# The state's unit moved to the end of its group in the first part of a two-part attention kernel

## The chip, the cores and the metric

The kernel runs on one core of one Trainium2 chip. The metric is the device time of one execution in microseconds (us), the median of several. The core has TensorE (PE in the profile, with its weight loads as PEld), VectorE (DVE), ScalarE (ACT) and GpSimd (POOL); SyncE (SP) only issues DMAs here.

## The reference

The program adds three things: its input x, a linear attention over the layer-normed x, and a two-layer windowed transformer over the same. The change is in the linear attention only (8 sequences of 1024 tokens, 16 heads, 16 features a head):

```python
q = taylor_feature_map(q)      # [1, x/2, x*x/(4*sqrt 2), x_i*x_j/4]
k = taylor_feature_map(k)
kv = jnp.cumsum(k[..., None, :] * v[..., :, None], axis=2)
y = jnp.einsum('bhtD,bhtdD->bhtd', q, kv)
z = jnp.cumsum(k, axis=2)
denom = jnp.sum(q * z, axis=-1, keepdims=True) + EPS
y = y / denom
```

The feature map makes q.k a polynomial, so y can be had in two ways: by squared scores between tokens ("near", causal), or by a state, a small matrix summed over all tokens of the past that each later token is multiplied with.

## The kernel before

Two blocks run one after the other: `taylor_block` (0 to about 870 us of the span) and `transformer_block` (the rest, untouched). In `taylor_block` a batch is one sequence. PE, DVE, ACT, POOL and SP each have a program written out by hand, in a fixed order, tied by semaphores. A batch has a projection (`project`) and then `attention`, which takes its 16 heads in four groups (`GROUPS`, `GH`) of four heads; below, the groups of a batch are the first to the fourth.

A group is a list of 14 units (`UNITS`). Each unit takes a pair of PSUM banks, out of three pairs in turn (`RING = 3`, `unit_bank`), so a unit can start on PE only when the unit three places before it has been emptied (`consumed`). The units are

- ten "near" units (steps 0 to 4, two heads each): PE makes scores (L843), ACT squares them into `weights` (L687), DVE masks the diagonal blocks of each step (`mask_diagonals`, L464);
- one "state" unit (L801 on PE): the state of the first four tiles, out of `psi`. POOL writes the pair products into `psi` (`pairs`, L344), DVE the squares and the constant (`other_rows`, L492 to L501), ACT the linear rows (`linear_rows`, L664). DVE copies the state out (`keep_state`, L471), PE turns it (`turn_state`, L809 and L811) into the second bank of the unit, and DVE copies that out in two pieces (`turn_state`, L478 and L479). Only then are the unit's banks free (`state_ready`);
- two "past" units (L838), squared on ACT (L687), and one "rest" unit (L831), squared on ACT (L680).

Four units behind the scores PE multiplies a finished step's weights with the values (`attend`: L859 for the steps 0 to 4, L866 and L869 for the step of the past), one step after each last unit of a step. `psi` is written anew for each group, so POOL, DVE and ACT wait for `state_ps` (the state's last matmul) before they write it for the next group.

The units' numbers in a group, from 0, before: near 0 to 9, state 10, past 11 and 12, rest 13. Three places behind the state is the rest unit, so the rest unit waits for `state_ready`.

Two more things hang on this order. SP loads the heads of the fourth group (`load_heads`, 12 DMAs) behind `invert(b, 0)`, which waits for a reciprocal on DVE (`invert_den`, L397) that stands at the end of the second group's DVE program, behind `turn_state` and `other_rows`. And PE's first unit of a group waits for its heads to have landed (`qkT_in`).

Of the kernel before, what the change touches and what calls it, by code (L numbers as in the profile page):

```python
# [27 lines left out]
GROUPS, GH = 4, 4  # L28
# [7 lines left out]
FORMS = P + VP  # L36
# [26 lines left out]
def taylor_block(nc, B, x, wqk, wv, wo, ident, causal, earlier, eps_rows, keep_rows, forms, own_head, later, xn_d, attn_d, parts_d, xnT_d,  # L63
                 id_s, ao, rot, qks_s, last_stored):

    with ExitStack() as ctx:
# [3 lines left out]
        def sem(name):  # L70
# [35 lines left out]
        state_T = small[:, 0:FORMS]  # L106
# [71 lines left out]
        NS = len(STEPS)  # L178
# [2 lines left out]
        PIECE = SEQ // 4  # L181

        UNITS = [(kind, i, pair) for kind, i, pair in
                 [("near", i, pair) for i in range(NS) for pair in range(2)] + [("state", NS, 0)] +
                 [("past", NS, pair) for pair in range(2)] + [("rest", NS, 0)]]
        NU = len(UNITS)
        SQUARES = NU - 1

        def squares_to(n):
# [9 lines left out]
        def unit_bank(n):  # L199
            return 2 + 2 * (n % RING)  # L200
# [169 lines left out]
        def _(dve):  # L370
# [77 lines left out]
            def attention(b, following):  # L448
                def add_before(g, half):

                    tiles = slice(half * TILES // 2, (half + 1) * TILES // 2)
                    if g == 0 and half == 0:
                        dve.wait_ge(before_ready, b + 1)
                    dve.wait_ge(pv_done, (b * GROUPS + g) * AS + LAST_STEP[half] + 1)
                    v.tensor_tensor(yT[:, g, half * 512:(half + 1) * 512].rearrange("p (t n) -> p t n", n=P),
                                    ps[:, half, :].rearrange("p (t n) -> p t n", n=P),
                                    before[:, g, tiles].unsqueeze(2).to_broadcast([P, TILES // 2, P]), ALU.add).then_inc(yT_ready, 1)

                def mask_diagonals(g, i):
                    w = GH * ((g * AS + i) % RING)  # L460
                    dve.wait_ge(squared, (b * GROUPS + g) * SQUARES + 2 * i + 2)
                    for o, width in DIAGONALS[i]:
                        a = weights[:, w:w + GH, o:o + width]
                        last = v.scalar_tensor_tensor(a, a, 16.0, causal_s[:, 0:width].unsqueeze(1).to_broadcast([P, GH, width]),  # L464
                                                      ALU.add, ALU.mult)
                    last.then_inc(diag, 1)

                def keep_state(g):
                    group = b * GROUPS + g
                    dve.wait_ge(state_ps, group + 1)  # L470
                    v.tensor_copy(state_T, ps[:, unit_bank(g * NU + 2 * NS), 0:FORMS]).then_inc(state_kept, 1)  # L471

                def turn_state(g):
                    group, bank = b * GROUPS + g, unit_bank(g * NU + 2 * NS) + 1
                    dve.wait_ge(turned_ps, group + 1)
                    if group:
                        dve.wait_ge(pv_done, group * AS)
                    v.tensor_copy(state_main, ps[:, bank, 0:P])  # L478
                    v.tensor_tensor(state_rest, ps[:, bank, P:2 * P], own_s[:, 0:P], ALU.mult).then_inc(state_ready, 1)  # L479

                def other_rows(g):

                    group = b * GROUPS + g
                    if g == 0:
                        dve.wait_ge(krows_ready, PAST * (b + 1))
                        for half in parts_out:
                            dve.wait_ge(half, 16 * (BLOCKS // 2) * (b + 1))
                    if group:
                        dve.wait_ge(state_ps, group)
                    k = krows[:, g].rearrange("p t h d -> p (t h) d")  # L490
                    squares = psi[:, :, ROW_SQUARES:ROW_SQUARES + TD]
                    v.reduce_sum(ksum[:, :], k, AX).then_inc(ksum_ready, 1)  # L492
                    dve.wait_ge(ksum_ready, 4 * group + 1)
                    v.tensor_scalar_add(ksum[:, :], ksum[:, :], 1.0).then_inc(ksum_ready, 1)
                    dve.wait_ge(ksum_ready, 4 * group + 2)
                    v.scalar_tensor_tensor(squares, k, 2.0, ksum[:, :].unsqueeze(2).to_broadcast([P, PAST * GH, TD]), ALU.mult, ALU.subtract)\
                        .then_inc(ksum_ready, 1)
                    v.tensor_scalar(psi[:, :, ROW_ONE:FORMS], ksum[:, :].unsqueeze(2).to_broadcast([P, PAST * GH, FORMS - ROW_ONE]),
                                    -1.0 / (FORMS - ROW_ONE), 3.0 / (FORMS - ROW_ONE), ALU.mult, ALU.add).then_inc(ksum_ready, 1)
                    dve.wait_ge(ksum_ready, 4 * group + 4)  # L500
                    v.tensor_tensor(squares, squares, k, ALU.mult).then_inc(psi_rest, 1)  # L501

                for g in range(GROUPS):
                    mask_diagonals(g, 0)
                    if g >= 1:
                        add_before(g - 1, 1)
                    mask_diagonals(g, 1)
                    if following is not None and g <= 1:
                        for t in range(4 * g, 4 * g + 2):
                            tile_stats(following, t)  # L510
                    if following is not None and g >= 2:
                        layer_norm(following, 2 * (g - 2))
                        layer_norm(following, 2 * (g - 2) + 1)
                    if g >= 2:
                        spread_den(b, g - 2)
                    mask_diagonals(g, 2)
                    if following is not None and g <= 1:
                        for t in range(4 * g + 2, 4 * g + 4):
                            tile_stats(following, t)
                    if following is not None and g == 1:  # L520
                        variances(following)
                    if g >= 2:
                        keep_den(b, g - 2)
                    if g == 0:
                        other_rows(0)
                    mask_diagonals(g, 3)
                    keep_state(g)
                    mask_diagonals(g, 4)
                    turn_state(g)
                    add_before(g, 0)  # L530
                    if following is not None and g % 2 and b >= len(later):
                        scale_tables((b - len(later)) * 2 + g // 2)
                    if g + 1 < GROUPS:
                        other_rows(g + 1)
                    if g >= 1:
                        invert_den(b, g - 1)
                add_before(GROUPS - 1, 1)
                if following is not None:
                    for t in range(TILES // 2, TILES):
                        layer_norm(following, t)  # L540
                spread_den(b, GROUPS - 2)
                keep_den(b, GROUPS - 2)
# [25 lines left out]
        def _(act):  # L568
# [98 lines left out]
            def attention(b):  # L667
                first = b * GROUPS * AS
                for n in range(GROUPS * NU):
# [5 lines left out]
                    if kind == "rest":  # L675
# [2 lines left out]
                        if first + s >= AS:  # L678
                            act.wait_ge(pv_done, first + s - AS + 1)
                        a.activation(rest_w, ps[:, bank, :], ACT.Square, bias=own_s[:, P:P + 1]).then_inc(squared, 1)  # L680
                        if n // NU + 1 < GROUPS:
                            linear_rows(b, n // NU + 1)
                    else:
                        if pair == 0 and first + s >= RING:
                            act.wait_ge(pv_done, first + s - RING + 1)
# [2 lines left out]
                                     bias=four_s[:, :] if kind == "near" else zero_s[:, :]).then_inc(squared, 1)  # L688
                    if n == 5:
                        linear_rows(b, 0)  # L690

            project(0)
            for b in range(B - 1):
# [7 lines left out]
        def _(pe):  # L701
# [81 lines left out]
            def attention(b):  # L783
# [19 lines left out]
                    last.then_inc(state_ps, 1)  # L803

                def turn_state(g):
                    bank = unit_bank(g * NU + 2 * NS) + 1
                    pe.wait_ge(state_kept, b * GROUPS + g + 1)
                    for r in range(0, P, VP):
                        mm(ps[r:r + VP, bank, 0:P], state_T[:, r:r + VP], id_s[:, :], start=True, stop=True)  # L809
                    for r in range(0, P, VP):  # L810
                        last = mm(ps[r:r + VP, bank, P:2 * P], state_T[:, P:P + VP], id_s[:, :], start=True, stop=True)  # L811
                    last.then_inc(turned_ps, 1)

                def scores(n):
# [6 lines left out]
                        pe.wait_ge(before_ready, b + 1)  # L821
                    if n % NU == 0:
                        pe.wait_ge(qkT_in[g % 2], 16 * 2 * SLOTS * (2 * b + g // 2 + 1))
                    if b == 0 and n == 2 * NS + 1:
                        pe.wait_ge(forms_set, 1)
                    if kind == "state":
                        state(n)
# [47 lines left out]
                last_of = {}  # L875
                for n in range(units):
                    kind, i, pair = UNITS[n % NU]
                    last_of[n // NU, i] = n
                ends = {n: step for step, n in last_of.items()}
                for n in range(units + BEHIND):  # L880
                    if n < units:
                        scores(n)
                    if n - BEHIND in ends:
                        attend(*ends[n - BEHIND])
                    if n % NU == 2 * NS + 1 and n < units:
                        turn_state(n // NU)

            project(0)
# [953 lines left out]
```

## Time and profile before

| | |
|---|---|
| median of 3 runs | 3475.45 us (3474.73 to 3481.47) |
| profiled execution, its own time | 3475.38 us |
| its span | 3473.6 us |
| PE busy | 3330.0 us, 96% of the span |
| ACT, DVE, POOL busy | 2518.9, 2736.3 and 1536.3 us |
| mean granted TensorE clock | 0.991 of full speed |

The spans are of one execution. A busy matmul row includes the tail of its last matmul, so two rows that follow without a wait overlap by 0.15 to 0.2 us; the distance of two starts is the truer length. In the timeline a row merges neighbouring instructions of one kind, and shows in brackets how long the engine was idle before it and who released it.

### The profile page before, as it was taken

To read this page: it belongs to the slowest core of one execution; us is meant where nothing else is said; L and a number is where in the kernel's file an instruction comes from. 1 tells how busy PE (TensorE), PEld (TensorE's weight loads), DVE (VectorE), ACT (ScalarE), POOL (GpSimd) and SP (SyncE) were. 2 spreads that over 40 slices of the span, in tenths; PEclk is the share of its full clock that TensorE was granted. 3 is DMA by queue.
4 is the path that set the end of the run, shared out by engine and by line. 5 is a ranking of instruction groups with operands and counts; after the bars stand their busy time and mean duration, and the time that the engine had idled before them with its cause. 6 is when DMAs were issued, how large, how long until landed. Compare 5 with 4: busy or idle time off the path is not lost.

```text
span 3473.6 us, 96643 instructions
## 1 busy us (share of the span) xinstructions
PE 3330.0 (96%) x36960; PEld 2498.5 (72%) x36960; DVE 2736.3 (79%) x8256; ACT 2518.9 (73%) x5629; POOL 1536.3 (44%) x1547
## 2 busy tenths in 40 slices
PE   7898889887799999999999999999999999999999
PEld 4555545554588787788788788888788888888887
DVE  4767777777688888888888888888888888888886
ACT  5667776666577777777777777777777777777775
POOL 4444444444444444444444444444444444444443
PEclk9999999999899999999999999999999999999999
DMA  6756676654422222222222222222222222222211
GB/s 159 174 128 139 126 154 144 141 100 87 134 63 62 73 66 62 73 67 62 73 66 62 73 67 62 73 66 62 73 68 62 72 67 62 72 69 62 71 45 43
DMA packets 289965, 293.94 MB, mean 85 GB/s; under 512 B 40960, under 2 KB 221536, under 8 KB 288992
## 3 DMA queue, kind: packets, MB, share of 16 engines
q1 hardware_dynamic: 289504, 287.74, 34.7%
q8 instruction: 295, 4.83, 0.6%
q14 instruction: 166, 1.36, 0.1%
HBM read 104.89 MB, written 58.73 MB: 47 GB/s over the span
## 4 chain that ended last, share of the span: by engine, by line
PE 73%; DVE 1%; POOL 0%; ACT 0%; issue 0%; DMA 0%; SPq 0%; DVEq 0%; POOLq 0%
PE f_ps L1575 19%; PE f_ps L1683 16%; PE f_ps L1695 10%; PE f_ps L1660 6%; PE f_ps L1639 4%; PE f_ps L1580 3%; PE f_ps L1602 3%; PE f_ps L1620 3%; PE f_ps L1649 2%; PE f_ps L1609 2%; PE f_ps L1688 2%; PE f_ps L1624 2%; PE f_ps L1667 1%; PE f_ps L1561 0%; ACT pr L1491 0%
## 5 line engine op out<-in xcount | busy, mean ns | idle before, releaser
L1246 POOL TENSOR_TENSOR turned<-qk,rot 128x256 f32<-128x256 f32 x512 | 405.4, 813 | 1250.5 <-ACT qk L1458 1235.4
L1575 PE MATMUL f_ps<-wqkv_s,hT 128*128 128x512 f32 x1536 | 707.2, 596 | 8.9 <-DMA hT<-xnT_dram 5.5
L1683 PEld LDWEIGHTS f_ps<-hnT,w_s 128*128 128x128 f32 x5120 | 591.7, 192 | 63.0 <-issue 59.8
L1326 DVE CUSTOM_DVE_ANT_0 pr<-f_ps,masks_s 128x192 f32<-128x192 f32 x1024 | 326.4, 355 | 360.7 <-PE f_ps L1609 358.7
L1683 PE MATMUL f_ps<-hnT,w_s 128*128 128x128 f32 x5120 | 592.5, 275 | 2.5 <-DVE hnT L1383 2.5
L1491 ACT ACTIVATE pr<-pr,nmax,rnorm 128x192 f32<-128x192 f32 x1024 | 545.0, 535 | 44.4 <-DVE nmax L1333 44.4
L1575 PEld LDWEIGHTS f_ps<-wqkv_s,hT 128*128 128x128 f32 x1536 | 276.9, 191 | 273.6 <-issue 186.7
L1343 DVE TENSOR_SCALAR pr<-pr,rsum 128x192 f32<-128x192 f32 x1024 | 445.4, 497 | 9.0
L1695 PE MATMUL f_ps<-w_s,act_u 128*128 128x256 f32 x1536 | 352.7, 379 | 0.0
L687 ACT ACTIVATE weights<-t_ps,four_s 128x1024 f32<-128x1024 f32 x320 | 326.4, 1132 | 26.1 <-PE t_ps L843 26.1
L1253 POOL TENSOR_TENSOR rnorm<-ssq,f_mhalf 128x8 f32<-128x8 f32 x128 | 255.7, 1998 | 163.9 <-DVE ssq L1303 163.9
L1695 PEld LDWEIGHTS f_ps<-w_s,act_u 128*128 128x128 f32 x1536 | 281.9, 190 | 33.0
L1480 ACT ACTIVATE kT<-f_ps 128x512 f32<-128x512 f32 x128 | 76.4, 597 | 293.6 <-PE f_ps L1580 293.6
L1515 ACT ACTIVATE act_u<-f_ps,b_s 128x128 f32<-128x128 f32 x640 | 205.1, 364 | 105.1 <-PE f_ps L1688 90.2
L464 DVE SCALAR_TENSOR_TENSOR weights<-weights,causal_s 128x512 f32<-128x512 f32 (+1 forms) x192 | 200.3, 1058 | 94.6 <-ACT weights L687 94.3
L1660 PE MATMUL f_ps<-fwo_s,oT 128*128 128x256 f32 x1024 | 242.4, 380 | 0.4 <-ACT oT L1504 0.4
L1293 DVE TENSOR_TENSOR cosine<-qk,rot 128x512 f32<-128x512 f32 x256 | 209.3, 818 | 12.1 <-ACT qk L1458 11.6
L1393 DVE SCALAR_TENSOR_TENSOR act_u<-f_ps,b_s,act_u 128x128 f32<-128x128 f32 (+1 forms) x768 | 208.4, 340 | 6.7 <-ACT act_u L1515 4.2
L1260 POOL TENSOR_TENSOR rnorm<-ssq,f_mhalf 128x8 f32<-128x8 f32 x128 | 209.0, 1633 | 0.0
L843 PE MATMUL t_ps<-qkT 96*32 96x512 bf16 (+3 forms) x4096 | 177.0, 307 | 31.8 <-ACT weights L687 17.2
L1310 DVE TENSOR_TENSOR qk<-cosine,turned 128x512 f32<-128x512 f32 x256 | 206.7, 808 | 0.3 <-issue 0.3
L843 PEld LDWEIGHTS t_ps<-qkT 96*32 96x32 bf16 x4096 | 98.2, 98 | 144.2 <-issue 61.6
(151 smaller groups left out, 6873.5 us busy)
## 6 DMA issues: line engine op xcount, KB each, us to landing
vw<-vw SPq DMA_DIRECT2D x628, 128.0 KB, 2.5
qkT<-parts_dram SPq DMA_DIRECT2D x384, 128.0 KB, 5.7
kT<-kT SPq DMA_DIRECT2D x124, 256.0 KB, 2.7
parts_dram<-shared SPq DMA_DIRECT2D x64, 384.0 KB, 3.1
xnT_dram<-xnT SPq DMA_DIRECT2D x8, 1025.0 KB, 5.4
xs<-x_dram SPq DMA_DIRECT2D x8, 1024.0 KB, 7.4
xn_dram<-xn SPq DMA_DIRECT2D x8, 1024.0 KB, 5.0
attn_dram<-ao SPq DMA_DIRECT2D x8, 1024.0 KB, 9.6
```

The lines of the kernel that those rows point to most:

```text
L687: a.activation(weights[:, w:w + 2, :], ps[:, bank:bank + 2, :], ACT.Square, bias=four_s[:, :] if kind == "near" else zero_s[:, :]).then_in ...
L843: last = mm(ps[r:r + VP, bank + k, o:o + 512 - c], qkT[g % 2][:, 1, h, j * P + r:j * P + r + VP], qkT[g % 2][:, 0, h, half * 512 + c:(half ...
L1246: g.tensor_tensor(turned[:, heads, f], qk[:, heads, z], sines, ALU.mult).then_inc(done, 1)
L1253: g.tensor_tensor(rnorm[:, HEADS:], ssq[:, HEADS:], mhalf[:, HEADS:], ALU.pow).then_inc(knorm_ready, 1)
L1293: v.tensor_tensor(cosine[:, heads, :], qk[:, heads, :], table, ALU.mult).then_inc(done, 1)
L1326: last = v.tensor_tensor_reduce(out=chances(h), in0=ps[:, SCORES[p], k * 256:k * 256 + BAND], in1=mask_of(it)[:, HALF - k * HALF:HALF - k ...
L1343: last = v.tensor_scalar_mul(chances(h), chances(h), rsum[:, h:h + 1])
L1491: last = a.activation(chances(h), chances(h), ACT.Exp, bias=nmax[:, h:h + 1], scale=rnorm[:, h:h + 1], accum_out=psum[:, h:h + 1])
L1575: last = mm(ps[:, b, :], rows, wqkv_s[:, l, c, i * INNER:(i + 1) * INNER], start=(c == 0), stop=(c == KC - 1))
L1660: last = mm(ps[:, WO, 0:DIM], oT[:, c, :], wo_s[:, l, c, :], start=(c == 0), stop=(c == INNER // P - 1))
L1683: last = mm(ps[:, UP[j // 2], o:o + P], w1_s[:, l, c, half * FULL + j * P:half * FULL + j * P + P], hnT[:, c, :], start=(c == 0), stop=(c ...
L1695: last = mm(ps[:, DOWN, 0:DIM], act_u[:, j, :], w2_s[:, l, j, :], start=(j == 0), stop=(j == FB - 1))
```

## The change

The state's unit moves from place 10 to place 13, behind the past and rest units, and is counted as a step of its own. So past is 10 and 11, rest is 12. Three places behind the state is now the third unit of the next group. `turn_state` on PE follows the same unit's slot, behind the last near `attend`, and `attend` of the past comes one place earlier, behind the third near unit of the next group. On DVE `keep_state` comes behind `add_before(g, 0)`. On ACT the linear rows of a group are copied behind the second unit of that group, no longer behind the rest unit of the group before.

```diff
         UNITS = [(kind, i, pair) for kind, i, pair in
-                 [("near", i, pair) for i in range(NS) for pair in range(2)] + [("state", NS, 0)] +
-                 [("past", NS, pair) for pair in range(2)] + [("rest", NS, 0)]]
+                 [("near", i, pair) for i in range(NS) for pair in range(2)] + [("past", NS, pair) for pair in range(2)] +
+                 [("rest", NS, 0), ("state", AS, 0)]]
         NU = len(UNITS)
+        STATE = NU - 1
...
                     mask_diagonals(g, 3)
+                    mask_diagonals(g, 4)
+                    add_before(g, 0)
                     keep_state(g)
-                    mask_diagonals(g, 4)
                     turn_state(g)
-                    add_before(g, 0)
...
                         a.activation(rest_w, ps[:, bank, :], ACT.Square, bias=own_s[:, P:P + 1]).then_inc(squared, 1)
-                        if n // NU + 1 < GROUPS:
-                            linear_rows(b, n // NU + 1)
...
                     if n == 5:
                         linear_rows(b, 0)
+                    if n >= NU and n % NU == 1:
+                        linear_rows(b, n // NU)
...
                     kind, i, pair = UNITS[n % NU]
-                    last_of[n // NU, i] = n
+                    if kind != "state":
+                        last_of[n // NU, i] = n
                 ends = {n: step for step, n in last_of.items()}
                 for n in range(units + BEHIND):
                     if n < units:
                         scores(n)
                     if n - BEHIND in ends:
                         attend(*ends[n - BEHIND])
-                    if n % NU == 2 * NS + 1 and n < units:
+                    if n % NU == STATE and n < units:
                         turn_state(n // NU)
```

In the rows of the changed kernel the lines stand one higher (L801 is L802, L843 is L844), but for ACT's square of the near and past units (L687 is L686).

On PE, from the state's unit of the first group to the second group's first attend of the past, before:

```order
L801 MATMUL t_ps<-shared,vals 32x160 x16
L838 MATMUL t_ps<-qkT,forms_s 32x512 x8
L859 MATMUL t_ps<-weights,vals 32x256 x8
L809 MATMUL t_ps<-id_s,shared 32x128 x4
L811 MATMUL t_ps<-id_s,shared 32x128 x4
L838 MATMUL t_ps<-qkT,forms_s 32x512 x8
L831 MATMUL t_ps<-qkT,forms_s 32x512 x4
L859 MATMUL t_ps<-weights,vals 32x384 x4
L859 MATMUL t_ps<-weights,vals 32x128 x4
L843 MATMUL t_ps<-qkT 32x512 x32
L866 MATMUL t_ps<-weights,shared 32x512 x4
L869 MATMUL t_ps<-shared 32x512 x4
```

and the same stretch in the changed kernel:

```order
L839 MATMUL t_ps<-qkT,forms_s 32x512 x16
L860 MATMUL t_ps<-weights,vals 32x256 x8
L832 MATMUL t_ps<-qkT,forms_s 32x512 x4
L802 MATMUL t_ps<-shared,vals 32x160 x16
L860 MATMUL t_ps<-weights,vals 32x384 x4
L860 MATMUL t_ps<-weights,vals 32x128 x4
L810 MATMUL t_ps<-id_s,shared 32x128 x4
L812 MATMUL t_ps<-id_s,shared 32x128 x4
L844 MATMUL t_ps<-qkT 32x512 x24
L867 MATMUL t_ps<-weights,shared 32x512 x4
L870 MATMUL t_ps<-shared 32x512 x4
L844 MATMUL t_ps<-qkT 32x512 x8
```

State (L802) and turn (L810, L812) now stand between the last scores of the group (L832) and the first of the next (L844); the same instructions are there in both.

On DVE, the end of the second group, from the masks of its steps 3 and 4 to the reciprocal, before:

```order
L464 SCALAR_TENSOR_TENSOR weights<-weights,causal_s 128x4x128 x2
L471 COPY shared<-t_ps 128x160
L464 SCALAR_TENSOR_TENSOR weights<-weights,causal_s 128x4x256
L478 COPY shared<-t_ps 128x128
L479 TENSOR_TENSOR shared<-t_ps,own_s 128x128
L455 TENSOR_TENSOR yT<-t_ps,before 128x512
L492 TENSOR_REDUCE ksum<-krows 128x16
L494 TENSOR_SCALAR ksum<-ksum 128x16
L496 SCALAR_TENSOR_TENSOR shared<-krows,ksum 128x16x16
L498 TENSOR_SCALAR shared<-ksum 128x16x8
L501 TENSOR_TENSOR shared<-shared,krows 128x16x16
L397 RECIPROCAL den_flat<-den_flat 128x32
```

and changed:

```order
L465 SCALAR_TENSOR_TENSOR weights<-weights,causal_s 128x4x128 x2
L465 SCALAR_TENSOR_TENSOR weights<-weights,causal_s 128x4x256
L456 TENSOR_TENSOR yT<-t_ps,before 128x512
L472 COPY shared<-t_ps 128x160
L479 COPY shared<-t_ps 128x128
L480 TENSOR_TENSOR shared<-t_ps,own_s 128x128
L493 TENSOR_REDUCE ksum<-krows 128x16
L495 TENSOR_SCALAR ksum<-ksum 128x16
L497 SCALAR_TENSOR_TENSOR shared<-krows,ksum 128x16x16
L499 TENSOR_SCALAR shared<-ksum 128x16x8
L502 TENSOR_TENSOR shared<-shared,krows 128x16x16
L398 RECIPROCAL den_flat<-den_flat 128x32
```

The mask of step 4 and the add to `yT` moved ahead of the three copies of the state; the rows for the next group (L493 to L502) and the reciprocal still stand behind them.

## Rows read from the trace of the kernel before

**Rows 1.** Waits, 0 to 870 us: waiting engine and line <- releaser: total us, times, longest.

```profile
PEld t_ps L831 <- DVE shared L479: 31.2, 31, 2.3
PE t_ps L843 <- DMA qkT<-parts_dram: 14.0, 7, 5.8
```

**Rows 2.** Timeline of PE, fourth batch, second group to the fourth's start: start, length, instructions.

```profile
380.04 1.48 PE L843 MATMUL t_ps<-qkT 96*32 96x512 bf16 x24
...
389.24 1.26 PE L801 MATMUL t_ps<-shared,vals 128*32 128x160 f32 x32
390.33 0.61 PE L838 MATMUL t_ps<-qkT,forms_s 96*32 96x512 bf16 x8
...
391.85 0.43 PE L809 MATMUL t_ps<-id_s,shared 128*32 128x128 f32 x8
...
392.29 0.65 PE L838 MATMUL t_ps<-qkT,forms_s 96*32 96x512 bf16 x8
...
393.33 1.04 PE L859 MATMUL t_ps<-weights,vals 128*32 128x384 f32 x16
394.19 1.47 PE L843 MATMUL t_ps<-qkT 96*32 96x512 bf16 x24
...
410.68 0.61 PE L843 MATMUL t_ps<-qkT 96*32 96x512 bf16 x8 [1.87 <-DMA qkT<-parts_dram]
```

**Rows 3.** Timeline of ACT, the same second group.

```profile
380.70 10.15 ACT L687 ACTIVATE weights<-t_ps,four_s 128x1024 f32<-128x1024 f32 x10 [0.89 <-PE t_ps L843]
...
394.56 0.41 ACT L664 ACTIVATE shared<-krows 128x256 f32<-128x256 f32 x1
```

**Rows 4.** Timeline of DVE, the end of the same group.

```profile
392.56 0.29 DVE L478 COPY shared<-t_ps 128x128 f32<-128x128 f32 x1 [0.34 <-PE t_ps L811]
...
393.56 0.41 DVE L492 TENSOR_REDUCE ksum<-krows 128x16 f32<-128x256 f32 x1
...
396.11 0.35 DVE L397 RECIPROCAL den_flat<-den_flat 128x32 f32<-128x32 f32 x1
```

**Rows 5.** Timeline of PE, fifth batch, first group and the second's start.

```profile
467.21 1.48 PE L843 MATMUL t_ps<-qkT 96*32 96x512 bf16 x24
...
482.71 0.40 PE L831 MATMUL t_ps<-qkT,forms_s 96*32 96x512 bf16 x4 [1.42 <-DVE shared L479]
...
483.80 0.39 PE L843 MATMUL t_ps<-qkT 96*32 96x512 bf16 x3
```

**Rows 6.** Timeline of DVE, the same first group: masks of steps 3 and 4.

```profile
477.49 1.29 DVE L464 SCALAR_TENSOR_TENSOR weights<-weights,causal_s 128x512 f32<-128x512 f32 x2
...
479.42 2.84 DVE L464 SCALAR_TENSOR_TENSOR weights<-weights,causal_s 128x1024 f32<-128x1024 f32 x1
```

**Rows 7.** Timeline of POOL, the same stretch.

```profile
479.22 5.31 POOL L344 TENSOR_TENSOR shared<-krows 128x1024 f32<-128x1024 f32 x7 [3.64 <-PE t_ps L801]
```

**Rows 8.** Timeline of DVE, fifth batch, third group: mask of step 3.

```profile
508.80 1.82 DVE L464 SCALAR_TENSOR_TENSOR weights<-weights,causal_s 128x512 f32<-128x512 f32 x2
```

**Rows 9.** Timeline of PE, fifth batch, fourth group, to the next projection.

```profile
515.30 1.48 PE L843 MATMUL t_ps<-qkT 96*32 96x512 bf16 x24 [1.03 <-DMA qkT<-parts_dram]
...
530.25 1.06 PE L866 MATMUL t_ps<-weights,shared 128*32 128x512 f32 x8 [0.30 <-ACT shared L680]
...
532.11 0.66 PE L711 MATMUL t_ps<-id_s,xn 128*128 128x128 f32 x4
```

**Rows 10.** Timelines of PE: attention's first unit in batches two, six and eight.

```profile
153.41 0.83 PE L843 MATMUL t_ps<-qkT 96*32 96x512 bf16 x12
...
570.71 0.62 PE L843 MATMUL t_ps<-qkT 96*32 96x512 bf16 x8
...
784.40 0.83 PE L843 MATMUL t_ps<-qkT 96*32 96x512 bf16 x12
```

**Rows 11.** Windows, PE alone: stretch, us, busy (x), granted clock, DMA share, GB/s.

```profile
411.40:414.80 3.40, 3.40 (x32) 0.50 0.05 10
```

**Rows 12.** Timeline of PE, second batch, second group: idle without a releaser.

```profile
184.83 0.42 PE L859 MATMUL t_ps<-weights,vals 128*32 128x256 f32 x3 [2.76 <-issue]
```

More of the change, by code:

```diff
@@ L470, in keep_state @@
                     dve.wait_ge(state_ps, group + 1)
-                    v.tensor_copy(state_T, ps[:, unit_bank(g * NU + 2 * NS), 0:FORMS]).then_inc(state_kept, 1)
+                    v.tensor_copy(state_T, ps[:, unit_bank(g * NU + STATE), 0:FORMS]).then_inc(state_kept, 1)
                 def turn_state(g):
-                    group, bank = b * GROUPS + g, unit_bank(g * NU + 2 * NS) + 1
+                    group, bank = b * GROUPS + g, unit_bank(g * NU + STATE) + 1
                     dve.wait_ge(turned_ps, group + 1)
@@ L805, in turn_state @@
                 def turn_state(g):
-                    bank = unit_bank(g * NU + 2 * NS) + 1
+                    bank = unit_bank(g * NU + STATE) + 1
                     pe.wait_ge(state_kept, b * GROUPS + g + 1)
@@ L823, in scores @@
                         pe.wait_ge(qkT_in[g % 2], 16 * 2 * SLOTS * (2 * b + g // 2 + 1))
-                    if b == 0 and n == 2 * NS + 1:
+                    if b == 0 and n == 2 * NS:
                         pe.wait_ge(forms_set, 1)
```

## The prediction

> **What bounds the kernel now.** I read the waits of the first part, then PE's timeline over whole groups, then ACT's and DVE's beside it, and last the starts of the batches. The waits name the target: PE's loads for the rest unit stand 31.2 us in 31 of 32 groups for DVE's second copy of the turned state, and beside it PE waits 14.0 us in 7 places for the heads of a group [rows 1]. The first number is idle time of the load path; it is not yet time of a batch.
>
> A group without disturbance lasts 394.19 - 380.04 = 14.15 us [rows 2]. ACT squares the ten near units without a pause in 10.15 us, about 1.00 each with a tail of 0.12 [rows 3]; with two past units at 1.0, the rest unit at 0.6 and the linear rows at 0.3 (starts of the next instruction: 394.56 to the next square at 394.86) it needs some 13.1 us. PE has no more than 14.15 less its waits, about 13.0 us. So both are nearly full, and what decides is in which order they hand over. Groups start as follows: the fourth group of batch four waits 1.87 us for its heads and that of batch five 1.03 us [rows 2, 9]. The heads' loads are issued behind the reciprocal at 396.11 to 396.46, and the group starts at 410.68, 14.22 us later [rows 2, 4]. So the time from the second group's end to the fourth group's start is a chain through DVE's reciprocal and SP's loads, not through PE.
>
> **What the change costs and gives, group by group.** No instruction is added or taken away; only places move. I lay the rows end to end for one batch.
>
> *First group.* Before, 483.80 - 467.21 = 16.59 us, with 1.42 us of it in PE's wait for the state [rows 5]. The wait was long because DVE's mask of step 4 took 2.84 us beside POOL's pair products, which start as soon as the state is done [rows 6, 7], and the copies of the turned state stood behind it. Now that mask is ahead of the state, when POOL is idle. What is late next: the mask of step 3 ends at 477.49 + 1.29 = 478.78 [rows 6]. Behind it on PE come attend of step 3 (0.87), the rest unit (0.22), the state 390.33 - 389.24 = 1.09, attend of step 4 394.19 - 393.33 = 0.86 and the turn 392.29 - 391.85 = 0.44 [rows 2]: 3.5 us, so the second group starts at 482.3, after 15.1 us. Gain 1.5 us.
>
> *Second group.* The state now needs the bank pair of the first past unit, and everything of the next group stands behind the state. From the first scores: 0.66 to ACT's first square (380.04 to 380.70), 0.30 for the linear rows that are now between squares, 10.15 for the ten, 1.0 for the first past unit, 0.06 to PE, then 1.09 + 0.86 + 0.44 [rows 2, 3]: 14.6 us. Before, the same group took 14.15. The state's wait is gone (the turned state has two units' time, 0.87, and needs about 0.8: 0.27 from the turn's end to DVE's copy at 392.56, and the two copies), but ACT now starves through state, attend and turn. Loss 0.4 us.
>
> *Third group.* Its length is set by the load chain. DVE's first copy stands 0.27 us behind the turn's end in both [rows 2, 4]. Now the turn's end is also the group's start; `other_rows` (393.56 here, [rows 4]) comes 0.4 behind that copy, so 0.67 after the start where it was 0.63 ahead of it. From there to the reciprocal's end 396.46 - 393.56 = 2.9 us, since POOL's products run beside it as here. So the reciprocal ends 3.6 us after the third group's start, before it was 396.46 - 394.19 = 2.3. With 14.2 for the loads: 17.8 us, before 410.68 - 394.19 = 16.49. Loss 1.3 us. PE's own work of the group would be done at 14.6, so PE idles some 3 us for the heads where it had 1.87. The bounds of the delay: 1.3 at least (the order alone, POOL as before), and 2.6 if the first small operations are held up as mask 4 was, by 1.5 us [rows 6].
>
> *Fourth group.* Before, 532.11 - 515.30 = 16.81 us [rows 9]. Now 14.6 as above, and DVE's masks are later here: that of step 3 takes 1.82 us instead of 1.29 beside POOL [rows 6, 8] and the linear rows push the squares behind which DVE's other work stands; I put 0.5 for it. At the end nothing hides the turned state: 0.8, and then attend of the past, 532.11 - 530.25 = 1.86 [rows 9]. Together 17.7. Loss 0.9 us, between 0.3 and 1.3.
>
> **The sum.** 15.1 + 14.6 + 17.8 + 17.7 = 65.2 us for attention in a batch. Before, batch five took 532.11 - 467.21 = 64.90, and its whole period 570.71 - 467.21 = 103.50; the mean period over batches two to seven is (784.40 - 153.41) / 6 = 105.17 [rows 5, 9, 10], so the mean attention is 64.90 + 1.67 = 66.57. The difference holds two kinds of accident that 65.2 does not. One is PE idle without a releaser, 2.76 us in batch two [rows 12]; I see seven over 0.6 us in the eight batches, which made the second groups longer. They fall while the heads of the third group still land. I add 0.7 a batch, between 0 (they hide in ACT's backlog, now that the loads start earlier in the group) and 1.2. The other is the clock: behind the 1.87 us wait for heads PE ran 3.40 us at 0.50 of the clock, the lower level of 1.2 GHz [rows 11], which costs up to 1.7 us. That happened at 3 of the 8 fourth groups, with waits of 1.17 us and more; with 3 us of wait I expect it in 6 of 8, 1.4 each, so 1.1 a batch. That makes 67.0 against 66.57, and 8 x 0.4 = 3.5 us more. The profiled execution took 3475.38 us, and the median of the runs is 3475.45, so the forecast is 3479 us. The second part is not touched. It starts behind the last batch's tail, which moves with its fourth group; that is in the sum.
>
> The Trainium skill (SBUF — State Buffer, section "SBUF: two separate sides") says that VectorE and GpSimd share one pair of ports under an exclusive lock: an operation with two SBUF inputs blocks for the whole of the other engine's instruction. The 2.84 us mask agrees in kind [rows 6, 7]. By that rule the first mask of the next group could be held until POOL's 5.31 us are over, some 4.3 us after the group's start, and then be just late for its attend at 4.6; the sum would rise by up to 0.5 us a group.
>
> The Trainium skill (TensorE: Matmul & The Clock Gate, section "HAM oscillation — how this bites in real kernels") warns that a wait for a DMA in every pass of a loop lets the clock fall each time. The trace shows it in three of eight; by the rule it would be all eight, 2.8 us more in the sum.
>
> **The rivals.**
> *The load chain and the clock take more than the first group gives (slower).* Mechanism: DVE's reciprocal of the second group stands behind the copies of the turned state, so the fourth group's heads are late by 2 us instead of 1.3, and each wait is followed by half clock. Price: 0.7 + 0.35 a batch on top, and 0.4 for later masks: 1.4 x 8 = 11, so 3490 us. It decides from a reciprocal that ends more than 4 us after the group's start. For it: the chain has no slack in 7 places [rows 1]. Against: the small operations behind POOL took 2.9 us in all here [rows 4].
> *The gain stays (faster).* The accidents of the second group vanish, since the loads of the third group's heads are asked for 2 to 3 us earlier against PE, and the clock does not fall oftener: 65.2 + 0.5 = 65.7 a batch, 0.9 x 8 = 7 us less, and with the fourth group at its lower bound 12: 3464 to 3468 us. For it: the first group's 1.5 us are sure to reach the reciprocal. Against: the third group gives it back.
> *The wait only moves.* The third near unit of the next group now waits for the state's banks with a slack of 0.1 us (0.87 against 0.8). If DVE is late by 0.5 us there, PE waits in 24 groups: 12 us on top of the 65.2, less what ACT's starving hides, about 3485 us.
>
> **How the numbers follow.** No change that can be measured (within 0.2%, 7 us, which is about what a measurement of this kernel can tell) 0.43; the slower chain 0.30; the moved wait 0.07; the faster case 0.20. So faster 0.20, same 0.43, slower 0.37. The likeliest has 3472 to 3482. The range for 8 in 10 takes most of both sides, 3466 to 3491: below it lies the fourth group's lower bound together with no accidents, above it half clock at each fourth group and the 2.6 us delay.
>
> **What would show it.** In the changed profile the wait of the rest unit for DVE is gone, and none is at the third near unit. Second groups without an accident take 14.6 us, with ACT idle 1.5 us before each group's first square. First groups take 15.1. The reciprocal ends 3.6 us after the third group's start, and PE's wait for heads rises from 14.0 us to about 25. The fourth group takes 17.7 at full clock. I am wrong if the fourth group's start comes earlier against the batch's start by more than 1 us on the mean, or if DVE's masks, not ACT, set the state's start.

## The result: slower by 0.4%

| | before | changed |
|---|---|---|
| median | 3475.45 us (5 runs, 3468.55 to 3481.47) | 3488.51 us (5 runs, 3486.41 to 3493.75) |
| span of the profiled execution | 3473.6 us | 3484.6 us |

The ratio is 1.004, 95% interval 1.0024 to 1.0056, so 8 to 19 us more. The page of the changed kernel shows the same counts of instructions and slightly less work on DVE and ACT; the mean granted clock is 0.990 where it was 0.991:

```profile
PE 3341.7 (96%) x36960; PEld 2506.9 (72%) x36960; DVE 2720.8 (78%) x8256; ACT 2513.1 (72%) x5629; POOL 1528.3 (44%) x1547
```

The waits of the first part, changed kernel (0 to 870 us). The wait of the rest unit for DVE (31.2 us, [rows 1]) is gone, and what is left of it at the third unit is on the load path only; the wait for heads has doubled:

```profile
PE t_ps L844 <- DMA qkT<-parts_dram: 27.7, 9, 5.0
PEld t_ps L844 <- DVE shared L480: 3.4, 15, 0.2
```

PE's timeline, fourth batch, from the end of its first group to the start of its fourth (answers to [rows 2]):

```profile
380.97 1.07 PE L860 MATMUL t_ps<-weights,vals 128*32 128x256 f32 x16 [1.07 <-DVE weights L465]
381.83 0.43 PE L832 MATMUL t_ps<-qkT,forms_s 96*32 96x512 bf16 x4
382.05 1.30 PE L802 MATMUL t_ps<-shared,vals 128*32 128x160 f32 x32
383.13 1.08 PE L860 MATMUL t_ps<-weights,vals 128*32 128x384 f32 x16
384.00 0.43 PE L810 MATMUL t_ps<-id_s,shared 128*32 128x128 f32 x8
...
384.43 1.51 PE L844 MATMUL t_ps<-qkT 96*32 96x512 bf16 x24
...
399.18 1.51 PE L844 MATMUL t_ps<-qkT 96*32 96x512 bf16 x24
...
416.68 0.61 PE L844 MATMUL t_ps<-qkT 96*32 96x512 bf16 x8 [2.70 <-DMA qkT<-parts_dram]
```

The second group takes 399.18 - 384.43 = 14.75 us where it took 14.15, the third 17.50 where it took 16.49. ACT at the border of the first two groups: behind the rest unit's square it waits 2.14 us for the first scores, in place of 0.89 [rows 3]:

```profile
382.30 0.69 ACT L681 ACTIVATE shared<-t_ps,own_s 128x512 f32<-128x512 f32 x1
385.12 2.12 ACT L686 ACTIVATE weights<-t_ps,four_s 128x1024 f32<-128x1024 f32 x2 [2.14 <-PE t_ps L844]
```

DVE at the third group's start, 399.18 (answers to [rows 4]). The turned state is copied at 399.45, the reciprocal ends at 402.57, 3.39 us into the group; PE gets the heads 14.1 us behind it:

```profile
399.45 0.29 DVE L479 COPY shared<-t_ps 128x128 f32<-128x128 f32 x1 [0.97 <-PE t_ps L812]
...
400.80 0.82 DVE L497 SCALAR_TENSOR_TENSOR shared<-krows,ksum 128x256 f32<-128x256 f32 x1
...
402.23 0.34 DVE L398 RECIPROCAL den_flat<-den_flat 128x32 f32<-128x32 f32 x1
```

The fourth group of the fifth batch (answers to [rows 9]), and the clock at its start:

```profile
521.15 2.60 PE L844 MATMUL t_ps<-qkT 96*32 96x512 bf16 x24 [2.70 <-DMA qkT<-parts_dram]
...
538.01 1.07 PE L867 MATMUL t_ps<-weights,shared 128*32 128x512 f32 x8 [0.70 <-DVE shared L480]
...
539.87 0.66 PE L712 MATMUL t_ps<-id_s,xn 128*128 128x128 f32 x4
```

```profile
521.40:524.80 3.40, 3.40 (x32) 0.50 0.03 5
```

The table has the mean lengths of the groups over the eight batches, read as distances of such starts in one trace each. (Batch eight has no projection behind it; its fourth group is counted to the end of its last matmul, less the tail.) "Bubbles" are PE's idle times over 0.3 us that have no releaser, summed between 52 and 862 us. "Half clock" is the time in us that PE was granted 0.50 of its clock, up to the end of the last batch's groups, without the 6.8 us that every kernel has at the first batch's start. The projection between two batches takes 38.6 us in every kernel.

| | first | second | third | fourth | a batch | bubbles | half clock |
|---|---|---|---|---|---|---|---|
| before | 16.94 | 15.80 | 16.13 | 17.36 | 66.2 | 10.4 | 23.9 |
| changed | 15.60 | 15.40 | 18.13 | 18.68 | 67.8 | 4.0 | 34.1 |

Where the expectations below speak of 12.2 us of bubbles before, they count a wait of 1.8 us at 816.14 among them, which the profile puts down to DVE.

67.8 - 66.2 = 1.6 us in eight batches is 12.7 us. It is in the third and fourth groups: 2.0 and 1.3 us lost, 1.3 and 0.4 won in the first two.

### The profile page after: what moved, and what is told of

Its sections match the earlier page's. It is cut to its first block, busy times and chain, and to the rows that moved or that the text cites. A ratio compares the mean times of both kernels' runs of the same rounds, so it can differ in the third digit from the quotient of the medians.

```text
span 3484.6 us, 96643 instructions
## 1 busy us (share of the span) xinstructions
PE 3341.7 (96%) x36960; PEld 2506.9 (72%) x36960; DVE 2720.8 (78%) x8256; ACT 2513.1 (72%) x5629; POOL 1528.3 (44%) x1547
## 4 chain that ended last, share of the span: by engine, by line
PE 73%; DVE 1%; POOL 0%; ACT 0%; issue 0%; DMA 0%; SPq 0%; DVEq 0%; POOLq 0%
PE f_ps L1577 19%; PE f_ps L1685 16%; PE f_ps L1697 10%; PE f_ps L1662 6%; PE f_ps L1641 4%; PE f_ps L1582 3%; PE f_ps L1604 3%; PE f_ps L1622 3%; PE f_ps L1651 2%; PE f_ps L1611 2%; PE f_ps L1690 2%; PE f_ps L1626 2%; PE f_ps L1669 1%; PE f_ps L1563 0%; ACT pr L1493 0%
## 5 line engine op out<-in xcount | busy, mean ns | idle before, releaser
L686 ACT ACTIVATE weights<-t_ps,four_s 128x1024 f32<-128x1024 f32 x320 | 329.7, 1130 | 91.2 <-PE t_ps L844 91.2
L465 DVE SCALAR_TENSOR_TENSOR weights<-weights,causal_s 128x512 f32<-128x512 f32 (+1 forms) x192 | 180.1, 957 | 108.6 <-ACT weights L686 107.6
L844 PE MATMUL t_ps<-qkT 96*32 96x512 bf16 (+3 forms) x4096 | 189.1, 310 | 43.7 <-DMA qkT<-parts_dram 27.7
L844 PEld LDWEIGHTS t_ps<-qkT 96*32 96x32 bf16 x4096 | 103.8, 98 | 161.7 <-ACT weights L686 70.2
## 6 DMA issues: line engine op xcount, KB each, us to landing
attn_dram<-ao SPq DMA_DIRECT2D x8, 1024.0 KB, 10.2
```

The lines of the kernel that those rows point to most:

```text
L686: a.activation(weights[:, w:w + 2, :], ps[:, bank:bank + 2, :], ACT.Square, bias=four_s[:, :] if kind == "near" else zero_s[:, :]).then_in ...
L844: last = mm(ps[r:r + VP, bank + k, o:o + 512 - c], qkT[g % 2][:, 1, h, j * P + r:j * P + r + VP], qkT[g % 2][:, 0, h, half * 512 + c:(half ...
```

## The experiments

The theory is the load chain: DVE's reciprocal at the end of the second group gates SP's loads of the fourth group's heads; the change puts the reciprocal later. The rivals are ACT starving at the border of the groups, the moved ACT copy, and loads that are late by themselves.

**The reciprocal moved, in either kernel (e1, e2).**

```diff
                     mask_diagonals(g, 3)
+                    if g >= 1:
+                        invert_den(b, g - 1)
                     mask_diagonals(g, 4)
...
-                    if g >= 1:
-                        invert_den(b, g - 1)
```

(in e2 it stands behind `keep_state`, directly ahead of the same mask.)

> The changed kernel with one edit: DVE's reciprocal (invert_den) stands ahead of the mask of step 4, no longer behind the copies of the state and other_rows. Theory (load chain): the heads of the fourth group are then asked for behind the group's rest scores, about 2.5 us before the third group starts, and land 11 us into it, so PE's wait for them (27.7 us) goes and third groups fall from a mean of 18.1 us to about 14.8: 8 x 3.3 = 26 us. With the waits the half clock in 6 of 8 fourth groups goes, 1.4 us each, 8 us more. About 3488 - 34 = 3454 us. Rival (ACT starving at the group's border is the loss): the time stays above the kernel before, 3480 us or more, with third groups as long as now. Rival (the loads themselves are late, not their request): third groups stay at 17 us and more.

Measured 3458.26 us (3452.17 to 3461.33), ratio to the kernel before 0.9949 [0.9936, 0.9961]. That is 30 us below the changed kernel, from one DVE instruction of 0.34 us moved to another place in each group behind the first. No fourth group waits for heads; the only such wait left is at the start of the first batch:

```profile
PE t_ps L844 <- DMA qkT<-parts_dram: 4.6, 1, 4.6
```

```profile
390.05 1.51 PE L844 MATMUL t_ps<-qkT 96*32 96x512 bf16 x24
...
405.28 1.51 PE L844 MATMUL t_ps<-qkT 96*32 96x512 bf16 x24
```

The third group of batch four takes 15.23 us instead of 17.50; the mean is 15.20. Fourth groups fall to 17.56. Of the 3.7 us that a batch wins, 2.9 are in third groups and 1.1 in fourth groups. So the request for the heads was late, and not the loads by themselves, and ACT's starving is not the main loss.

> The kernel before with the same edit alone: the reciprocal ahead of the mask of step 4. Load chain: the waits for heads (14.0 us) go, third groups fall from 16.1 us to about 14.5, 13 us in all, and the half clock in 3 of 8 fourth groups goes, 4 us: about 3458 us. With e1 this tells what the new order of the units is worth without the load chain: by the rows (first group -1.3 us, second +0.4 where undisturbed, fourth +0.5) it comes out even, so e1 and e2 within 6 us of each other. Rival (the unit order is the real gain and only the chain hid it): e1 is 15 us or more below e2.

Measured 3478.67 us (3469.59 to 3482.70), ratio 1.001 [1.0001, 1.0019]: no gain, against 3458 expected. The waits for heads did go, but here the reciprocal stands too early. It waits for the denominators' DMA 16.4 us in 12 places, and the mask behind it meets POOL's products (2.07 us, where it takes 1.2 alone). DVE in the second group of batch five:

```profile
498.74 0.35 DVE L397 RECIPROCAL den_flat<-den_flat 128x32 f32<-128x32 f32 x1 [1.32 <-DMA den_flat<-yT]
499.01 2.07 DVE L464 SCALAR_TENSOR_TENSOR weights<-weights,causal_s 128x1024 f32<-128x1024 f32 x1
501.01 0.28 DVE L478 COPY shared<-t_ps 128x128 f32<-128x128 f32 x1
```

In the old order the state's copies stand behind that mask, so PE's rest unit pays: its weight loads wait 46.5 us for DVE instead of 31.2, and PE itself 29.4 us instead of 14.9. That is more than the 8.5 us of waits for heads that went.

```profile
PEld t_ps L831 <- DVE shared L479: 46.5, 32, 3.1
```

**The reciprocal behind the turned state, in either kernel (e5, e8).**

```diff
                     turn_state(g)
+                    if g >= 1:
+                        invert_den(b, g - 1)
```

> The kernel before with the reciprocal right behind the copies of the turned state, ahead of add_before and other_rows. In e2 the same instruction stood ahead of the mask of step 4 and waited 0.8 to 2.4 us there for the denominators' DMA (which lands behind the third group's heads), so the mask fell into POOL's products (2.02 us in second groups instead of 1.40). Here the denominators have landed. Load chain: the heads' wait of 14.0 us goes, third groups fall from 16.1 to about 14.7 us, half clock in fourth groups goes: 3475 - 11 - 4 = 3460 us. If e2 was level for another reason (the chain is not what bounds third groups before the change), this is level too, 3475 us.

Measured 3468.23 us (3463.29 to 3473.42), ratio 0.9977 [0.9967, 0.9987]: 8 us won where 15 were expected. No wait for heads is left behind the first batch's start, and no fourth group has half clock. Where nothing disturbs, third groups are as short as expected (14.47 to 14.63 us in batches one, two and eight). Most of what is missing is bubbles, 20.0 us of them in place of 10.4, and new ones in the third groups of batches three to seven, as here:

```profile
513.60 1.07 PE L859 MATMUL t_ps<-weights,vals 128*32 128x256 f32 x16 [1.21 <-issue]
```

> The changed kernel with the reciprocal right behind the copies of the turned state. It then ends about 1.1 us after the third group's start instead of 3.4 (5.4 in batches six and seven). Load chain: the third group takes 1.1 + 14.2 = 15.4 us, 2.7 less than the mean of now; 8 x 2.7 = 22 us, and fewer half clocks, up to 8 us: 3459 to 3466 us, so 0 to 8 us above e1. Rival (e1 won by something else, as the instruction's absence from the group's start): the same as e1 or lower.

Measured 3459.55 us (3456.88 to 3462.09), ratio 0.9951 [0.9938, 0.9963]. With the reciprocal's end 1.0 us into the third group its mean is 15.57 us, with the end 3.4 (twice 5.4) us into it 18.13, with the end 3.4 us ahead of it 15.20. The loads land 0.1 to 0.7 us before the fourth group starts, so the chain has just let go.

e5 and e8 have the reciprocal at the same place in the two orders, and here the new order is 9 us faster (3459.55 against 3468.23; the intervals of the two ratios do not touch). The traces have 20.0 us of bubbles in e5 and 6.9 in e8.

**The ACT part alone, and undone (e3, e4).**

```diff
-                        if n // NU + 1 < GROUPS:
-                            linear_rows(b, n // NU + 1)
...
+                    if n >= NU and n % NU == 1:
+                        linear_rows(b, n // NU)
```

> The kernel before with the change's ACT part alone: the linear rows of a group are copied behind its own second unit instead of behind the rest unit of the group before. The copy (0.3 us between squares) moves out of a place where ACT still has work waiting into the row of squares, which ACT runs without a pause, so it costs nothing or 0.3 us in second and fourth groups: 3475 to 3480 us. Rival (this part is the loss): 3485 us or more.

Measured 3478.43 us (3470.26 to 3481.79), ratio 1.0003 [0.9994, 1.0012]: no difference.

> The changed kernel with the ACT part undone: linear rows again behind the rest unit of the group before. In the changed order ACT is idle there about 1.5 us until the next group's first scores, and the state's last matmul ends before the rest square does, so the copy hides and the squares of the next group come 0.3 us earlier. Second and fourth groups win 0.3 us each, third groups also, since the chain to the reciprocal starts at the group's end: about 24 x 0.3 = 7 us, 3481 us. Rival (ACT then waits for the state in front of the copy and the first square is late): 3488 us or more.

Measured 3485.99 us (3485.63 to 3492.32), ratio to the kernel before 1.0035 [1.0023, 1.0048]; the changed kernel had 1.004. Undisturbed second groups fall from 14.75 to 14.45 us as expected, third groups do not (18.42 on the mean, bound by the heads). The time does not tell it from the changed kernel.

**On top of e1 (e6, e7, e9).** e6 is e1 with e4's edit.

> e1 with the linear rows back behind the rest unit. In e4 second groups went from 14.74 to 14.45 us, but third groups stayed bound by the heads. With the chain gone the 0.3 us should be had in 24 groups: 7 us, 3451 us. Rival (ACT is not what paces the groups, DVE is): 3458 us.

Measured 3452.65 us (3450.99 to 3454.92), ratio 0.9932 [0.9919, 0.9946]. That is the fastest of the kernels that compute everything, 24 us below the median of the kernel before in the same comparison (3476.69). The gain over e1 is the size that was expected, but the intervals of the two ratios overlap; the lengths of the groups say it more clearly: undisturbed second groups fall from 14.75 to 14.44 us and third groups from 15.0 to 14.3 or 14.4. So ACT sets the length of the undisturbed groups. Its ten squares are one row again:

```profile
490.20 0.42 ACT L665 ACTIVATE shared<-krows 128x256 f32<-128x256 f32 x1
491.91 10.16 ACT L688 ACTIVATE weights<-t_ps,four_s 128x1024 f32<-128x1024 f32 x10 [1.30 <-PE t_ps L844]
```

e7 turns the state behind the next group's first unit:

```diff
-                    if n % NU == STATE and n < units:
-                        turn_state(n // NU)
+                    if n % NU == 0 and NU <= n < units:
+                        turn_state(n // NU - 1)
+                    if n == units - 1:
+                        turn_state(n // NU)
```

> e1 with PE's turn of the state behind the next group's first unit instead of ahead of it (for the last group of a batch as before). ACT's first square comes 0.44 us earlier in 24 groups; the state's banks come free 0.44 us later, which the third unit then waits for, but ACT needs that unit only 2.3 us behind its first square. ACT starving at the border is the price of the new order: 24 x 0.4 = 10 us, 3448 us. Rival (the third unit's wait takes it back, since the attend of the past stands behind it on PE): 3458 us or more.

Measured 3460.63 us (3460.01 to 3462.51), ratio 0.9956 [0.9943, 0.9968]: the rival. The time alone does not settle it, as the trace has 12.9 us of bubbles against 5.9 in e1. In the rows of ACT, the first square comes 0.4 us earlier, and that is lost before the fourth, since PE does the third unit late and then the attend of the past:

```profile
510.90 1.11 ACT L686 ACTIVATE weights<-t_ps,four_s 128x1024 f32<-128x1024 f32 x1
512.39 7.14 ACT L686 ACTIVATE weights<-t_ps,four_s 128x1024 f32<-128x1024 f32 x7 [0.38 <-PE t_ps L844]
```

e9 is e6 with the first group's `other_rows` behind the mask of step 3:

```diff
                     mask_diagonals(g, 2)
...
-                    if g == 0:
-                        other_rows(0)
                     mask_diagonals(g, 3)
+                    if g == 0:
+                        other_rows(0)
```

> e6 with DVE's other_rows of a batch's first group behind the mask of step 3 instead of ahead of it. With the state last in its group those rows are needed a unit and a half later, and in the first groups PE waits about 1 us for the mask of step 3, as the prediction named it. First groups fall from 15.3 (median 15.55) to about 14.5 us: 8 x 0.8 = 6 us, 3446 us. Rival (the rows then hold up the mask of step 4 or the state, so PE waits there as long): level with e6, 3453 us.

Measured 3456.06 us (3451.71 to 3458.93), ratio 0.9937 [0.9922, 0.9951]: level with e6. Only two of eight first groups are free of bubbles. Batch four's takes 14.68 us, where 15.2 are the rule in e6; batch eight's takes 14.68 too, but had 14.60 in e6. So the gain is seen in one group only, and the trace has 12.3 us of bubbles instead of 7.2.

**Lighter loads (e10, e11).** Both leave three of four heads unloaded in half of the DMAs for third and fourth groups, so part of the scores comes from old values.

```diff
+                        hs = 1 if g >= 2 and i >= 3 else GH
-                        sp.dma_start(qkT[g % 2][i * TD:(i + 1) * TD, a, :, :],
-                                     parts_d[a, part, g * GH * TD:(g + 1) * GH * TD, :].rearrange("(h d) n -> d h n", d=TD))\
+                        sp.dma_start(qkT[g % 2][i * TD:(i + 1) * TD, a, 0:hs, :],
+                                     parts_d[a, part, g * GH * TD:(g * GH + hs) * TD, :].rearrange("(h d) n -> d h n", d=TD))\
```

> The kernel before, in which half of the DMAs for the heads of third and fourth groups carry one head of four (the rest of the values is left as it was), so these loads are shorter by a third. Load chain: the heads land 4 to 5 us earlier behind the reciprocal, the waits of fourth groups go (third groups 14.7 us where no bubble is). Bubbles (PE idle without a releaser, 12.2 us in this trace, 20.0 in e5 with its earlier loads): if they come from instructions that queue behind these loads, they fall too, to 8 us or less. Together 3475 - 11 - 4 = 3460 us or less. Rival (bubbles have nothing to do with the heads' loads): 12 us of them remain, about 3465 us.

Measured 3447.46 us (3446.39 to 3449.07), ratio 0.9915 [0.9895, 0.9934]. Waits for heads are 0.4 us at most behind the first batch's start, one bubble is left, 1.7 us, and behind the first batch's start no half clock. That is 12 us below what was expected. Second groups take 14.15 us in five of eight batches. Two starts of batch five:

```profile
471.17 0.39 PE L844 MATMUL t_ps<-qkT 96*32 96x512 bf16 x3
...
485.52 1.47 PE L844 MATMUL t_ps<-qkT 96*32 96x512 bf16 x24
...
500.00 1.47 PE L844 MATMUL t_ps<-qkT 96*32 96x512 bf16 x24
```

> The changed kernel with the same lighter loads (the same values left out) and the reciprocal where the change has it. Load chain: landing comes 3.4 + about 9.5 = 13 us after the third group's start, so the wait of 27.7 us goes though DVE's order is untouched, and the time falls to that of e1, 3455 to 3460 us. Rival (DVE's late reciprocal costs by itself, as by holding up the first mask of the group): 3475 us or more.

Measured 3455.76 us (3451.70 to 3458.91), ratio 0.9937 [0.9919, 0.9954], level with e1 with DVE's order untouched. The reciprocal still ends 3.4 to 5.4 us into the third group, and no fourth group waits for its heads. So it is the late landing of the heads that costs, not the reciprocal's place on DVE by itself. Bubbles are 5.6 us here, and there is no half clock behind the first batch's start.

The same table for the experiments that the verdict rests on:

| | first | second | third | fourth | a batch | bubbles | half clock |
|---|---|---|---|---|---|---|---|
| e1 | 15.62 | 15.67 | 15.20 | 17.56 | 64.1 | 5.9 | 13.7 |
| e5 | 16.89 | 15.97 | 15.96 | 16.85 | 65.7 | 20.0 | 10.2 |
| e8 | 15.82 | 15.10 | 15.57 | 17.71 | 64.2 | 6.9 | 3.4 |
| e6 | 15.66 | 15.47 | 15.08 | 17.15 | 63.4 | 7.2 | 10.2 |
| e10 | 16.67 | 14.37 | 14.71 | 16.92 | 62.7 | 1.7 | 0 |
| e11 | 15.66 | 15.23 | 15.17 | 17.56 | 63.6 | 5.6 | 0 |

From e10 to e11 the order of the units changes, with waits for heads of 0.4 us at most and no half clock in either. The new order wins 1.0 us in first groups and loses 0.9, 0.5 and 0.6 in the others. So with these lighter loads it is 8 us slower (3447 to 3456), of which 4 are bubbles. With full loads e5 and e8 say the opposite, and there the bubbles differ by 13 us. What the order alone is worth hangs on the bubbles, and no run here separates the two.

## Why the prediction was right, and where it was too small

The range held the time (3466 to 3491, measured 3488.5), but the forecast was "no change that can be measured", and the kernel is measurably slower. The mechanism of the slower rival, the load chain, was in the forecast too; it was undersized in the sum, not missing. Its price, 3490 us, is near what was measured. Over the eight batches the reciprocal ended 1.7 us into the third group before and 3.9 us in the changed kernel, so 2.2 us later where the sum had 1.3, and third groups became 2.0 us longer. From the reciprocal's end to the fourth group's start it took 14.4 us before and 14.2 after, as laid out. The signs came as named: the rest unit's wait is gone, the wait for heads is 27.7 us (about 25 forecast), and in batch four ACT waits 2.14 and 1.70 us ahead of the first square of the second and the third group (1.5 forecast).

*First group*, 15.1 us, mean 15.60. The wait moved to the mask of step 3 as said (1.07 us before L860). Undisturbed groups take 15.3: in batch four the mask ends 0.15 us later than laid out. The rest is in part bubbles of 0.45 and 0.75 us, and in part half clock in the first groups of batches one, two and seven (0.85 to 0.89 of the clock over the group), which the sum did not have. Batch five's 15.70 has neither and stays unexplained.

*Second group*, 14.6 and 0.7 for accidents, mean 15.40, undisturbed 14.75. ACT starving at the border was right, and e6 shows that ACT is what paces these groups.

*Third group*, 17.8, mean 18.13. Six batches have the reciprocal's end 3.4 to 3.5 us into the group (3.6 forecast) and take 17.0 to 17.9 us. Batches six and seven have it at 5.39 and take 19.7 and 20.3: there `scale_tables` stands between the copies and the reciprocal, four DVE operations that the sum left out:

```profile
610.22 2.57 DVE L551 TENSOR_TENSOR rot<-rot,qks_s 128x256 f32<-128x256 f32 x4
```

This is the term of the sum that failed, 0.5 us a batch. It stands there in the kernel before as well: in e10, which has the old order and hardly a bubble, the reciprocal ends 4.26 us into these two third groups and 2.26 us into most others. In the kernel before a bubble stands near the end of each of the two second groups (601.35 and 708.76), and the reciprocal ended 2.26 and 2.86 us into the third. The six other groups took 17.5 on the mean, a little under 17.8, so the mean of all is off by 0.33 only.

*Fourth group*, 17.7 and 1.1 for the clock, mean 18.68. At full clock it takes 17.33 (batch four) and 17.79 (batch eight); the three most alike of the others take 18.72. Half clock came in 6 of 8, as said, and costs 1.39 us in those three. The Trainium skill's warning (TensorE: Matmul & The Clock Gate, "HAM oscillation — how this bites in real kernels") holds in kind: six of these waits, of 2.1 to 4.3 us, have the clock at 0.50 behind them, and the waits of 2.70 and 2.07 us in batches four and eight do not.

*The base.* I took 66.57 us for a batch before, the mean of six; the mean of all eight is 66.22. That hides 2.8 us. With it and the third group's 0.33, the first's 0.5 and the second's 0.1, less 0.1 in the fourth, the forecast of 3.5 us becomes 12.8; the table has 12.7, and 13 were measured.

*The accidents.* I gave the changed kernel 0.7 us a batch for bubbles; the trace has 4.0 us in all. That it came out near in the sum is luck: batch two's second group took 18.68 us, with one bubble of 1.99 us and half clock behind it, and that one group holds 0.5 of the 0.7:

```profile
186.39 1.13 PE L802 MATMUL t_ps<-shared,vals 128*32 128x160 f32 x17 [1.99 <-issue]
```

```profile
186.80:190.20 3.40, 3.40 (x53) 0.51 0.02 5
```

The sum reckoned half clock behind waits for heads only. In the kernel before three of seven such stretches stand behind those waits and two behind bubbles. Of the seven bubbles over 0.6 us that it put into second groups, five stand there.

*The lock on the shared ports* (the Trainium skill, SBUF — State Buffer, "SBUF: two separate sides"): the mask of step 4 in first groups fell from a mean of 2.83 us to 1.22 once POOL's products no longer ran beside it. The first mask of the next group ran beside POOL's last product (402.49, the product from 402.43 to 403.26) and took 0.63 us, so in this place the trace does not show it held, and the rule's price for that mask did not come.

*What makes a bubble.* The traces of all thirteen kernels hint that PE's instructions come late. They have 98 bubbles, and 96 of them end 1.15 to 1.65 us behind the end of a 16 KB packet on the DMA queue that the profile calls "instruction"; such stretches behind a packet cover 5% of the time. In batch six of the kernel before the packet ends at 599.91 and PE goes on at 601.35:

```profile
601.35 0.30 PE L811 MATMUL t_ps<-id_s,shared 128*32 128x128 f32 x1 [1.56 <-issue]
```

No edit tested this. That the heads' loads bring the bubbles on is also not settled: lighter loads took them from 10.4 to 1.7 us in the old order, but in the changed order they stayed at 5.6 against 4.0 and 5.9, with one trace each.

## What to carry to other kernels

Before an instruction is moved past others on one engine, follow what is queued behind it there to the DMAs that it gates on another queue: one small reciprocal, 2.2 us later on the mean, cost more than the first groups had won, and moving it alone was worth 30 us. Place such an instruction where its own input has landed, not as early as possible. And when two engines pace a loop, a stall that is taken away comes back as the other engine's starving: count both at the border of the group.

## What the runs showed of the hardware

- PE stood without a releaser for 10.4 us in one trace and 20.0 us in another (e5), and 96 of 98 such times in all traces ended 1.15 to 1.65 us behind the end of a 16 KB packet on the instruction queue.
- The granted clock was at its lower level (0.50) behind waits for heads of 2.1 to 4.3 us in six of eight places of the changed kernel, and also behind a bubble of 1.99 us. With lighter loads (e10, e11) it did not fall between the first batch's start and the end of the last batch's groups.
- DVE copies out of PSUM (L478, L479) took 0.27 to 0.29 us also beside POOL's products, while masks in SBUF took up to 2.84 us instead of 1.2.
